# Inverse roots by Ln and Exp, two gates multiplied into weights, and first maxima taken on pairs of banks, in a two-layer adaLN transformer kernel

## The reference

```
x = x + ga * attention0(layernorm(x) * (1 + ca) + sa)     # windowed "light" attention + a routed "heavy" one
x = x + gb * ffn0(layernorm(x) * (1 + cb) + sb)           # 256 -> 64, 16 hidden units for each, -> 256
x = x + ga * attention1(layernorm(x) * (1 + ca) + sa)     # 16 heads of 16, causal over the 1024 tokens
x = x + gb * ffn1(layernorm(x) * (1 + cb) + sb)           # 256 -> 1024 -> 256, exact gelu, binarized weights
```

## Time and profile before

| | |
|---|---|
| median of 3 runs | 4067.61 us (4062.26 to 4075.77) |
| profiled execution | 4068.53 us, span 4066.8 us |
| PE / DVE / ACT / POOL busy | 83% / 60% / 48% / 36% of the span |
| mean granted TensorE clock | 0.91 |

### The profile page before, as it was taken

How to read it: one execution, slowest core, us unless ns; L and a number is a source line. 1 busy time by engine, 2 the same in 40 slices (tenths; PEclk the granted TensorE clock), 3 DMA queues, 4 the chain that set the end, 5 groups by cost and what they waited for, 6 DMA issues and landing times. The chain is left out here.

```text
span 4066.8 us, 81863 instructions
## 1 busy us (share of the span) xinstructions
PE 3382.8 (83%) x30905; PEld 2021.9 (50%) x30905; DVE 2459.2 (60%) x6188; ACT 1955.7 (48%) x4555; POOL 1476.9 (36%) x1799
## 2 busy tenths in 40 slices
PE   7368778897799878998798977998788987998787
PEld 3235554564446544465545644465444654465444
DVE  6754767466563666547573675637674575736662
ACT  5224444544364544554455542654445543645434
POOL 4123452244423542235422543235422344235411
PEclk8579889998899989998899988999899988999888
DMA  6210230002300123002400023002220024000220
GB/s 235 84 37 14 56 106 28 14 12 64 110 16 25 32 64 84 23 12 56 117 17 14 28 51 108 17 24 55 77 56 16 12 64 111 16 25 21 59 69 7
DMA packets 233603, 207.39 MB, mean 51 GB/s; under 512 B 13776, under 2 KB 214224, under 8 KB 233176
## 3 DMA queue, kind: packets, MB, share of 16 engines
q1 hardware_dynamic: 229168, 192.61, 16.9%
q0 software_dynamic: 3328, 8.39, 0.8%
q10 hardware_dynamic: 720, 1.15, 0.1%
HBM read 123.83 MB, written 77.69 MB: 50 GB/s over the span
## 5 line engine op out<-in xcount | busy, mean ns | idle before, releaser
L2399 ACT ACTIVATE arena<-pb 128x512 f32<-128x512 f32 (+3 forms) x1536 | 663.9, 493 | 239.2 <-PE pb L1615 232.7
L2479 POOL TENSOR_TENSOR arena<-arena,small 128x512 f32<-128x512 f32 x256 | 287.8, 1126 | 475.6 <-DVE small L1791 474.1
L2223 ACT ACTIVATE arena<-arena,small 128x256 f32<-128x256 f32 x512 | 255.8, 500 | 381.0 <-DVE small L1774 380.6
L1573 PE MATMUL pb<-arena 96*32 96x128 bf16 (+5 forms) x5280 | 371.0, 278 | 67.0 <-DVE arena L2078 24.9
L1615 PE MATMUL pb<-arena 98*32 98x512 bf16 (+3 forms) x4608 | 399.7, 340 | 31.0 <-ACT arena L2399 23.1
L1633 PE MATMUL pb<-arena,v 128*17 128x512 f32 (+3 forms) x3072 | 379.3, 498 | 22.0 <-POOL arena L2643 13.7
L2643 POOL TENSOR_SCALAR_AFFINE_SELECT arena<-arena 128x256 f32<-128x256 f32 x512 | 217.3, 428 | 474.3 <-ACT arena L2399 470.5
L2078 DVE TENSOR_REDUCE arena<-pb 128x1 f32<-128x512 f32 x512 | 334.2, 684 | 85.7 <-PE pb L1573 83.4
L1774 DVE CUSTOM_DVE_ANT_0 arena<-pb,wmask 128x256 f32<-128x256 f32 x512 | 195.7, 419 | 214.5 <-PE pb L1310 201.8
L1573 PEld LDWEIGHTS pb<-arena 96*32 96x32 bf16 (+1 forms) x5280 | 183.8, 101 | 250.7 <-issue 62.9
L1310 PE MATMUL pb<-arena 128*128 128x256 f32 x1024 | 282.9, 401 | 5.0 <-issue 2.8
(11 more groups left out here) (339 smaller groups left out, 7123.6 us busy)
## 6 DMA issues: line engine op xcount, KB each, us to landing
arena<-split_q SPq DMA_DIRECT2D x64, 384.0 KB, 3.8
arena<-split_k SPq DMA_DIRECT2D x24, 768.0 KB, 6.7
split_q<-arena SPq DMA_DIRECT2D x64, 192.0 KB, 2.1
...
```

Source lines behind the costliest of these rows:

```text
L1573: mm = t.matmul(out[r:r + wide], qh[:, q0 + r:q0 + r + wide], kh_, **kw)
L2223: ins = s.activation(pm[n % 3][:, j], sm[n % 2][:, j], ACT.Exp, bias=nmx[:, 2 * sl + j:2 * sl + j + 1], scale=-1.0, accum_out=sml[:, 2 * s ...
L2399: s.activation(pp[pn % 4][:, h % 2, 0:w_], bank[n % 3][:, 0:w_], ACT.Exp).then_inc(a_exp1, 1)
L2479: g.tensor_tensor(pm[n % 3], pm[n % 3], rcl[:, 2 * sl:2 * sl + 2].unsqueeze(2).broadcast_to([P, 2, 2 * P]), ALU.mult).then_inc(p_norm0, 1)
```

## The change

Four things:

1. The inverse roots are ACT's: Ln with epsilon as its bias, then Exp with scale -1/2. DVE's addition and POOL's power go. This holds for both norms of `chain` and for `norm_half`.
2. POOL multiplies the gate into ffn0's output weights (`wfog`, once a batch in `hrows`) and into attention1's (`wo1g`, once a batch at the start of `att`). The PSUM result is then added to x by one DVE instruction, and POOL adds nothing.
3. The first fills use four banks, the pairs (0, 1) and (4, 5), and DVE reduces two fills with one instruction on two banks; the row of group 0 is turned in bank 2.
4. The names of semaphores follow; the steps of the schedule are the same.

```diff
@@ -253,6 +253,7 @@
 MAX_BANKS = (4, 5)
+FIRST_BANKS, FIRST_ROW_BANK = ((0, 1), (4, 5)), 2
...
@@ -1163,6 +1166,7 @@
 oc = view([TH, D])
+wo1g = [at(hTf, G1 * N // 2, [D]), wog[:, :]]
 nm = [view([G1, TH, 4]) for _ in range(2)]
...
@@ -1508,8 +1511,9 @@
 t.wait_ge(v_chain[j], nth(CHAIN_V, n, "g8"))
+t.wait_ge(p_const, 3 * (b + 1))
 for i in range(2):
-    mm = t.matmul(bank[bk][:, i * D:(i + 1) * D], L.gT[:, i * P:(i + 1) * P], wfo[:, :], start=True, stop=True)
+    mm = t.matmul(bank[bk][:, i * D:(i + 1) * D], L.gT[:, i * P:(i + 1) * P], wfog[:, :], start=True, stop=True)
 mm.then_inc(t_chain[j], 1)
...
@@ -1561,8 +1565,8 @@
-def fill(g, kind, h, wide=32):
-    bk = max_bank()
+def fill(g, kind, h, wide=32, no=None):
+    bk = max_bank() if no is None else FIRST_BANKS[no // 2 % 2][no % 2]
     for w in left[bk]:
...
@@ -1590,11 +1594,11 @@
     mx[0] += 1
-    left[bk] = [(v_mx, mx[0])]
+    left[bk] = [(v_mx, mx[0] + (1 - no % 2 if no is not None else 0))]
 def row_of(g):
     G = (2 * b + c) * NG + g
-    bk = max_bank()
+    bk = max_bank() if g else FIRST_ROW_BANK
     for w in left[bk]:
...
@@ -1648,7 +1652,7 @@
 for n, f in enumerate(first_fills(c)):
-    fill(*f, wide=P)
+    fill(*f, wide=P, no=n)
     if n == len(fills(c)):
...
@@ -1687,12 +1691,13 @@
 t.wait_ge(a_oc, 2 * (2 * b + c + 1))
+t.wait_ge(p_wo, b + 1)
 for i in range(TH):
     bk = 4 + i % 2
     for w in left[bk]:
         t.wait_ge(*w)
     for k in range(KD):
-        mm = t.matmul(bank[bk][:, 0:D], ocT[:, k, i * P:(i + 1) * P], wo1[:, k], start=k == 0, stop=k == KD - 1)
+        mm = t.matmul(bank[bk][:, 0:D], ocT[:, k, i * P:(i + 1) * P], wo1g[k], start=k == 0, stop=k == KD - 1)
     mm.then_inc(t_o1, 1)
...
@@ -1923,8 +1928,6 @@
 ins.then_inc(n_stat, 1)
-v.wait_ge(n_stat, 2 * H + 2)
-v.tensor_scalar(rs, mv[:, :, 1], 1e-5, None, ALU.add).then_inc(n_var, 1)
 yield
...
@@ -1960,11 +1963,9 @@
 ins.then_inc(done, 1)
-v.wait_ge(done, nth(CHAIN_V, n, op + "_ag"))
-v.tensor_scalar(L.rs, L.mv[:, :, 1], 1e-5, None, ALU.add).then_inc(done, 1)
-yield
-yield
-v.wait_ge(p_chain[j], nth(CHAIN_P, n, op + "_pow"))
+yield
+yield
+v.wait_ge(a_chain[j], nth(CHAIN_A, n, op + "_rs"))
 for i in range(2):
...
@@ -1989,11 +1990,11 @@
 v.wait_ge(t_chain[j], nth(CHAIN_T, n, "wfo"))
-v.tensor_tensor(L.xpair, bank[chain_bank(c, j, "wfo")].rearrange("p (t d) -> p t d", d=D), gates[:, 1].unsqueeze(1).broadcast_to([P, 2, D]),
-                ALU.mult).then_inc(done, 1)
-yield
-yield
-v.wait_ge(p_chain[j], nth(CHAIN_P, n, "xa"))
+v.wait_ge(p_chain[j], nth(CHAIN_P, n, "m_bi"))
+v.tensor_tensor(x, bank[chain_bank(c, j, "wfo")].rearrange("p (t d) -> p t d", d=D), x, ALU.add).then_inc(done, 1)
+yield
+yield
+v.wait_ge(done, nth(CHAIN_V, n, "xa"))
 yield from statistics("p")
...
@@ -2079,6 +2080,25 @@
+def fill_pair(g, kind, h, no):
+    G = (2 * b + c) * NG + g
+    bk = pb2[FIRST_BANKS[no // 2 % 2][0] // 2][:, :, :]
+    m = nm[g % 2]
+    if (kind, h) == fills(c)[0] and G >= 2:
+        v.wait_ge(v_nm, 2 * G - 3)
+    v.wait_ge(t_mx, mx[0] + 2)
+    if kind == "D":
+        ins = v.tensor_reduce(m[:, h:h + 2, :, 0], bk.rearrange("p b (i k) -> p b i k", k=P), AX_X, ALU.max)
+    elif kind == "E":
+        ins = v.tensor_reduce(m[:, h:h + 2, 2:4, 1], bk.rearrange("p b (i k) -> p b i k", k=2 * P), AX_X, ALU.max)
+    elif kind == "O":
+        ins = v.tensor_reduce(m[:, 0:4].rearrange("p h i s -> p h (i s)")[:, :, 5:15:9],
+                              bk.rearrange("p b (h j k) -> p (b h) j k", h=2, k=P), AX_X, ALU.max)
+    else:
+        ins = v.tensor_reduce(m[:, h:h + 2, int(kind[1]), 3], bk, AX_X, ALU.max)
+    ins.then_inc(v_mx, 2)
+    mx[0] += 2
+
 def parts_of(g, taken):
...
@@ -2117,7 +2135,8 @@
 for n, f in enumerate(first_fills(c)):
-    fill(*f)
+    if n % 2:
+        fill_pair(*first_fills(c)[n - 1], n - 1)
     if n == len(fills(c)) - 1:
...
@@ -2145,10 +2164,8 @@
 v.wait_ge(t_o1, t_ + 1)
-if i >= 2:
-    v.wait_ge(p_o1, t_ - 1)
-v.wait_ge(gate2_in, 16 * (b + 1))
-v.tensor_tensor(oc[:, i % 2], bank[4 + i % 2][:, 0:D], gates[:, 2], ALU.mult).then_inc(v_o1, 1)
+x = xt[:, TH * c + i]
+v.tensor_tensor(x, bank[4 + i % 2][:, 0:D], x, ALU.add).then_inc(v_o1, 1)
 yield
...
@@ -2310,7 +2327,15 @@
 H = 2 * b + c
-for _ in range(6):
+_, mv, rs = n_small()
+yield
+yield
+s.wait_ge(n_stat, 2 * H + 2)
+exp_tables()
+s.activation(rs, mv[:, :, 1], ACT.Ln, bias=eps5[:, 0:1]).then_inc(n_var, 1)
+s.wait_ge(n_var, H + 1)
+s.activation(rs, rs, ACT.Exp, scale=-0.5).then_inc(n_pow, 1)
+for _ in range(4):
     yield
...
@@ -2334,7 +2359,17 @@
-for _ in range(6):
+def inverse_root(op):
+    s.wait_ge(v_chain[j], nth(CHAIN_V, n, op + "_ag"))
+    exp_tables()
+    s.activation(L.rs, L.mv[:, :, 1], ACT.Ln, bias=eps5[:, 0:1]).then_inc(done, 1)
+    s.wait_ge(done, nth(CHAIN_A, n, op + "_ln"))
+    s.activation(L.rs, L.rs, ACT.Exp, scale=-0.5).then_inc(done, 1)
+
+for _ in range(3):
+    yield
+inverse_root("m")
+for _ in range(3):
     yield
...
@@ -2348,7 +2383,10 @@
     yield
-for _ in range(8):
+for _ in range(5):
+    yield
+inverse_root("p")
+for _ in range(3):
     yield
...
@@ -2510,6 +2548,7 @@
 g.tensor_tensor(gbias[:, 0], rows[:, R_BOUT:R_BOUT + D], gates[:, 1], ALU.mult).then_inc(p_const, 1)
+g.tensor_tensor(wfog[:, :], wfo[:, :], gates[:, 1], ALU.mult).then_inc(p_const, 1)
 yield
...
@@ -2553,13 +2592,7 @@
 def norm_half(b, c):
-    H = 2 * b + c
-    _, _, rs = n_small()
-    yield
-    yield
-    g.wait_ge(n_var, H + 1)
-    g.tensor_tensor(rs, rs, mhalf[:, 0:TH], ALU.pow).then_inc(n_pow, 1)
-    for _ in range(6):
+    for _ in range(8):
         yield
...
@@ -2579,8 +2612,6 @@
 yield
-g.wait_ge(v_chain[j], nth(CHAIN_V, n, op + "_ep"))
-g.tensor_tensor(L.rs, L.rs, mhalf[:, 0:2], ALU.pow).then_inc(done, 1)
 yield
...
@@ -2589,14 +2620,11 @@
 yield
-g.wait_ge(p_const, 2 * (b + 1))
+g.wait_ge(p_const, 3 * (b + 1))
 g.wait_ge(p_bias2, b + 1)
 yield from statistics("m", gbias[:, 0])
 for _ in range(12):
     yield
-g.wait_ge(v_chain[j], nth(CHAIN_V, n, "xa"))
-g.wait_ge(done, nth(CHAIN_P, n, "m_bi"))
-g.tensor_tensor(x, x, L.xpair, ALU.add).then_inc(done, 1)
 yield
...
@@ -2630,6 +2658,11 @@
 def att(b, c):
+    if c == 0:
+        g.wait_ge(t_qkv, sum(QKV_T) * (b + 1))
+        for k in range(KD):
+            ins = g.tensor_tensor(wo1g[k], wo1[:, k], gates[:, 2], ALU.mult)
+        ins.then_inc(p_wo, 1)
     for _ in first_fills(c):
...
@@ -2645,12 +2678,7 @@
 yield
-for k in range(KD):
-    yield
-for i in range(TH):
-    x = xt[:, TH * c + i]
-    g.wait_ge(v_o1, TH * (2 * b + c) + i + 1)
-    g.tensor_tensor(x, x, oc[:, i % 2], ALU.add).then_inc(p_o1, 1)
+for k in range(KD + TH):
     yield
```

More of the change, by code:

```diff
@@ L36 @@
 NH, TH = N // 2, T // 2
-ZONE_B = 13648
-ARENA = 22864
+ZONE_B = 13568
+ARENA = 22784
 MU, INNER = 64, 16
@@ L236 @@
 CHAIN_T = ("m_n2", "win", "wfo", "p_n2", "qk0", "qk1", "v", "sp0", "sp1")
-CHAIN_V = ("hadd", "m_st", "m_ag", "m_ep", "m_no") + tuple(f"g{j}" for j in range(INNER // 2 + 1)) + (
-    "xa", "p_st", "p_ag", "p_ep", "p_no", "v1", "hs", "ta0", "ta1", "ad0", "rs0", "r0", "ad1", "rs1", "r1", "rr0", "rr1")
-CHAIN_A = ("m_ev", "s") + tuple(f"l{j}" for j in range(INNER // 2)) + ("p_ev", "qc0", "qc1", "ln", "rs", "hi0", "mi0", "hi1", "mi1")
-CHAIN_P = ("m_pow", "m_bi", "xa", "p_pow", "p_bi", "qq0", "qq1", "ro0", "ro1", "lo0", "lo1")
+CHAIN_V = ("hadd", "m_st", "m_ag", "m_no") + tuple(f"g{j}" for j in range(INNER // 2 + 1)) + (
+    "xa", "p_st", "p_ag", "p_no", "v1", "hs", "ta0", "ta1", "ad0", "rs0", "r0", "ad1", "rs1", "r1", "rr0", "rr1")
+CHAIN_A = ("m_ln", "m_rs", "m_ev", "s") + tuple(f"l{j}" for j in range(INNER // 2)) + ("p_ln", "p_rs", "p_ev", "qc0", "qc1", "ln", "rs", "hi0", "mi0", "hi1", "mi1")
+CHAIN_P = ("m_bi", "p_bi", "qq0", "qq1", "ro0", "ro1", "lo0", "lo1")
 CHAIN_BANKS = {(0, 0): (5, 6), (0, 1): (7, 6), (1, 0): (6,), (1, 1): (7,)}
@@ L384, in adaln_kernel @@
         gbias = sb("gbias", [P, 2, D])
+        wfog = sb("wfog", [P, D])
+        wog = sb("wog", [P, D])
         small = sb("small", [P, 640])
@@ L1138, in adaln_kernel @@
             sem(n) for n in ("n_stat", "n_var", "n_pow", "n_out", "t_n2", "a_nx", "a_n2", "v_nx", "v_n2", "p_bias", "p_btmp"))
[L1140 removed]
+        ones_in, v_b3, t_mx, v_mx, v_nm, v_nms, t_row, v_row, t_s1, a_exp1, p_tri, t_pv1, a_og, t_og, v_rec1, v_oc, t_oc, a_oc, t_o1, v_o1, p_wo = (
             sem(n) for n in ("ones_in", "v_b3", "t_mx", "v_mx", "v_nm", "v_nms", "t_row", "v_row", "t_s1", "a_exp1", "p_tri", "t_pv1", "a_og",
[L1142 removed]
+                             "t_og", "v_rec1", "v_oc", "t_oc", "a_oc", "t_o1", "v_o1", "p_wo"))
         nullv_in = sem("nullv_in")
@@ L1915, in norm_half @@
                     for i in range(TH):
-                        v.wait_ge(p_o1, TH * H + i + 1)
+                        v.wait_ge(v_o1, TH * H + i + 1)
                         ins = v.bn_stats(st[:, i], xt[:, TH * c + i])
@@ L2097, in row_of @@
                             v.wait_ge(row_in[G % 2], 16 * (G // 2))
```

(10 more changed lines are left out.)

3 lines of the change are left out of this document (removed).

## The result

After takes 4030.9 us (median of 4 runs, 4027.5 to 4034.2), before 4068.8 (4 runs, 4062.3 to 4075.8): ratio 0.9905, 95% interval 0.9888 to 0.9922. That is 38 us less. The forecast was 4033, with 3990 to 4060 as its range. The profiled execution of after took 4027.5 us, its span 4025.5. Figures for a batch are read from one profiled execution of each kernel, and most of them from the six batches in the middle.

The account below looks back on a forecast made before the run. The prediction took TensorE's own work, busy 83% of the span, as the bound, so only its waits could be won. Its terms, -16.6 - 7 - 11 - 8 + 8, made -35 us: 4033 us, range 3990 to 4060.

Parts of the forecast that it names:

- Term 1: First half's norm_half: no waits for POOL's additions and a shorter root win 2.0 us a batch, -16.6 us in all.
- Term 2: First fills, first half: four banks and eight pair reductions for sixteen single ones win 0.9 us a batch, -7 us.
- Term 3: First fills, second half: four banks shorten TensorE's held fills by 1.55 us a batch, -11 us; bounds 0 and -25.
- Term 4: Norms of chain: without DVE's epsilon addition, slow beside POOL, 1.2 us a batch is won, -8 us; bounds 0 and -20.
- Term 5: 80 new Ln and Exp pairs on ACT delay its queue in three of ten places, 1.0 us a batch, +8 us.
- Rival C: Ln heads ACT's queue until DVE has aggregated, holding exponentials and evictions in light: slower, about 4109 us; chance 5%.
- B: Wins in the fills return as waits for the row's DMA or the scores' pace; 4055 us; chance 17%.
- A: In the thin stretches shorter waits also shorten TensorE's time at the lower clock; about 3990 us; chance 20%.
- D: One reduction over two banks costs 1.5 us, not 1.21: +9 us, 4042; chance 8% together with mixtures.

Follow-up runs that it names:

- pow_back: After with POOL's pow put back at each of the chains' 64 norms, its output unused: 4027.3 us, ratio 0.9895 to the kernel before.

## Why the prediction was right

The time was right, and most of the mechanism, but two errors of about the same size cancelled: the third term gave nothing where 11 us were forecast, the fourth 21 where 8 were. That the sum came within 3 us of the measured time is luck.

- **Term 1 (norm_half, -16.6): right.** The wait shrank by 2.31 us a batch, forecast 2.0, so about -18, estimated from the wait. That such a wait turns into time, the gates alone show: 1.56 us less wait a batch, 12 us less time. Both halves of it were seen: no wait for POOL, 0.60 us for the root (0.7 taken).
- **Term 2 (first fills, first half, -7): right in size.** 1.0 us a batch against 0.9, and 0.9 with the pairs alone. But the reason was incomplete: single reductions on the same four banks make 1.9 a batch (16.95 us, against 18.88 before). The banks give, the pairing takes back nearly half.
- **Term 3 (first fills, second half, -11): this step failed.** The waits went as forecast: that of 1.71 us is gone, and of that of 2.81 us 0.5 was won (forecast 0.7) and 2.28 stay. But I summed TensorE's idle time and left the clock out. TensorE idles 2.1 us a batch less and works 2.1 us a batch longer on the same matmuls; the stretch stayed at 445 us. The lower bound of that term, 0, was the result. Four banks with single reductions make the stretch 2.3 us a batch shorter than before (430.8 us against 444.7 in six), which the pairing hides.
- **Term 4 (norms of chain, -8): mechanism right, mis-sized.** It is the addition of epsilon, and it measured 21 us. I counted two places a batch from the trace (1.2 us). The light stages gave 1.95, and epsilon's return took 2.2, some 17 us in eight batches; the trace does not say where the other 4 us of the 21 lie. I had taken the short additions (0.17 us, each behind a wait for VectorE's own aggregation) as hidden behind VectorE's own queue. That they stand on the path is the likely reason for the excess, but no run puts only them back. The bound of -20 was reached. The other thing in that bound, POOL's pow out of POOL's queue, is worth nothing.
- **Term 5 (ScalarE's pairs, +8): agrees with a doubling (+7.4), not shown beyond the runs' uncertainty.** One reading behind it was off. It had every aggregation over before ScalarE gets there, or within 0.1 us; in 20 of the 64 places ScalarE stood idle until the aggregation, 32.1 us in all (row L2365 above). In eleven of the 20 its next instruction then waited for TensorE anyway, and TensorE's waits for ScalarE are in sum not longer than before (some 205 us against 210). Rival C, the queue's head, is excluded by the result and by the roots alone, 29 us faster. Doubling the pairs doesn't test it, since the second pair waits for nothing.
- **The rivals.** B (absorbed) came true for the second half's fills, through the clock and not through a DMA. A (the clock follows and adds to the win) had the wrong sign there: less idle time came with more time at 1.2 GHz. In the two thin stretches of the batch shown the clock fell too, from 0.68 to 0.66 and from 0.72 to 0.60. Only over six batches is there a little of it in the first half: from first fill to first score TensorE runs 12.0 us a batch at 1.2 GHz, against 13.9 before. D is out: 1.22 us.

With the measured sizes the sum is -18 - 8 + 0 - 21 + 7 = -40, against the -38 of the runs; the 7 is not clear of zero, and without it the sum is -47. For the roots alone the same terms, -21, +7, and their share of `norm_half` (wait 6.62 to 5.89, -6), make -20, against 29 measured (its interval reaches from -21 to -42). The 9 us between are unexplained. The mean clock of that kernel's five executions was 0.912 to 0.914, that of after's four 0.905 to 0.909, so the clock may have a part in them, which no run separates.

The Trainium skill ("SBUF — State Buffer", section "SBUF: two separate sides") had a rule against the fourth term: whichever of POOL and a VectorE instruction of certain kinds starts first holds the ports that they share, so the normalization that moves up would be held by POOL in its turn. The rows of after bear it out. Two normalizations take 1.39 us at 2802.78, beside POOL's L2655, which ends at 2803.29, and POOL's next instruction. In the kernel before they take 0.74 at the same place:

```profile
2829.85 0.74 DVE L1969 TENSOR_SCALAR xn<-xt,small 128x256 f32<-128x256 f32 x2 [0.77 <-POOL small L2583]
```

TensorE pays nothing for it there: its wait for the normalization is 0.27 us in after and 0.35 before.

What stays open: why the pairing goes with more time at the lower clock in the second half. That it does, the stretches from norm to first score show in all traces without unneeded matmuls. TensorE's busy time in six batches is 377 to 386 us in the six kernels with pairs there (its idle time 66 to 68), 365 to 373 in the four on two banks (idle 76 to 80), and 357 with single reductions on four banks (idle 73). A few us of such a figure are chance: it is 377 in after and 381 in `pow_back`, whose TensorE instructions are the same and whose time is not apart. Filling the norm's wait with matmuls doesn't undo it. Matmuls in the short waits of the second half's fills were not tried.
